# A new end, second-norm moments on VectorE and routing counts one step earlier, in an S4D plus mixture-of-experts kernel

## The reference

```python
x = x + _layernorm(_L0_attn_ref(_layernorm(x, axis=-1), ...), axis=-1)   # four S4D layers
x = x + _layernorm(_L0_ffn_ref(_layernorm(x, axis=-1), w1, w2, router_w), axis=-1)
```

## Time and profile before

| | us |
|---|---|
| median of the runs | 1039.69 |
| the three runs | 1039.56, 1039.69, 1178.92 |
| the profiled execution, device time | 1034.42 |
| its span, first to last instruction | 1032.6 |

### The profile page before, as it was taken

The page is one execution under the profiler, slowest core; times in us unless marked ns, Lnnn a source line. Parts: engine busy times, 40 slices in busy tenths (PEclk is TensorE's granted clock), DMA queues, the critical chain, the costliest instruction groups (busy, mean ns, idle before and its releaser), DMA issues.

```text
span 1032.6 us, 25421 instructions
## 1 busy us (share of the span) xinstructions
PE 689.0 (67%) x8355; PEld 594.1 (58%) x8356; DVE 746.7 (72%) x1806; ACT 574.8 (56%) x1249; POOL 553.6 (54%) x759
## 2 busy tenths in 40 slices
PE   0029438697677958789487888736999999990000
PEld 0018338675676738767386666635888898880000
DVE  8987866779675885759767599844778777773563
ACT  7627961069401792028700488824888888872544
POOL 2113314346441573415543277876777777777883
PEclk9999759899797988979798898557999999995555
DMA  7905699990999819995499400113555555542232
GB/s 282 397 0 161 201 386 388 330 385 4 312 387 324 303 48 358 384 329 205 140 361 403 176 1 1 62 52 118 163 165 168 167 161 168 163 143 56 79 97 74
DMA packets 123814, 209.13 MB, mean 203 GB/s; under 512 B 18892, under 2 KB 45784, under 8 KB 123096
## 3 DMA queue, kind: packets, MB, share of 16 engines
q1 hardware_dynamic: 115544, 191.28, 52.6%
q0 software_dynamic: 8192, 16.79, 5.6%
HBM read 168.97 MB, written 39.06 MB: 201 GB/s over the span
## 4 chain that ended last, share of the span: by engine, by line
POOL 30%; PE 28%; issue 26%; DVE 9%; ACT 4%; DMA 2%; POOLq 1%; SPq 0%; ACTq 0%; DVEq 0%
PE bank L1117 12%; POOL zbuf L561 7%; POOL toep L627 6%; PE bank L1132 6%; POOL rstd_of L550 6%; PE bank L970 3%; POOL z_sorted L613 3%; PE bank L948 2%; PE bank L1084 2%; POOL sums L541 1%; DMA toep<-kernels_dram 1%; POOL rstd_of L528 1%; POOL mean_of L546 1%; POOL m L548 1%; POOL shift_of L552 1%
## 5 line engine op out<-in xcount | busy, mean ns | idle before, releaser
L970 PE MATMUL bank<-zbuf,toep 128*128 128x128 f16 (+3 forms) x3328 | 145.4, 206 | 93.5 <-DVE zbuf L1327 72.2
L970 PEld LDWEIGHTS bank<-zbuf,toep 128*128 128x128 f16 x3328 | 142.0, 102 | 97.6 <-issue 50.6
L561 POOL TENSOR_TENSOR zbuf<-zbuf,w_cur 128x256 f32<-128x256 f32 x120 | 90.4, 755 | 141.2 <-DVE zbuf L1391 141.2
L613 POOL DMA_INDIRECT z_sorted<-toep x128 | 131.1, 1024 | 43.5 <-issue 35.3
L1117 PE MATMUL bank<-toep 128*128 128x256 f16 x1152 | 144.0, 275 | 3.1 <-issue 0.9
L1391 DVE TENSOR_REDUCE zbuf<-bank 128x256 f32<-128x512 f32 x128 | 86.9, 687 | 72.0 <-PE bank L970 72.0
L1005 PE MATMUL bank<-wo_cur,glu_work 128*128 128x256 f32 x512 | 135.6, 410 | 2.5 <-ACT glu_work L785 2.2
L785 ACT ACTIVATE glu_work<-bank,unscale_cur 128x512 f32<-128x512 f32 x64 | 42.7, 668 | 164.7 <-PE bank L992 164.6
L1117 PEld LDWEIGHTS bank<-toep 128*128 x1152 | 111.1, 99 | 22.3 <-issue 9.3
L1005 PEld LDWEIGHTS bank<-wo_cur,glu_work 128*128 128x128 f32 x512 | 97.2, 200 | 43.7 <-issue 17.8
L528 POOL TENSOR_TENSOR rstd_of<-var,neg_half 128x16 f32<-128x16 f32 (+1 forms) x16 | 37.6, 2352 | 106.8 <-DVE var L1187 106.6
(11 more groups left out here) (241 smaller groups left out, 1527.2 us busy)
## 6 DMA issues: line engine op xcount, KB each, us to landing
toep<-kernels_dram SPq DMA_DIRECT2D x104, 1024.0 KB, 14.0
glu_work<-kernels_dram SPq DMA_DIRECT2D x16, 1024.0 KB, 14.1
z_sorted<-ln_tmp SPq DMA_DIRECT2D x4, 3072.0 KB, 23.8
toep<-z_sorted SPq DMA_DIRECT2D x96, 128.0 KB
y_sorted<-toep SPq DMA_DIRECT2D x96, 128.0 KB
toep_last<-kernels_dram SPq DMA_DIRECT2D x8, 1024.0 KB, 14.2
hres<-in_x SPq DMA_DIRECT2D x1, 4096.0 KB, 13.0
toep<-in_x SPq DMA_DIRECT2D x1, 4096.0 KB, 23.9
```

The source lines that it names most:

```text
L561: G.tensor_tensor(y, y, w, ALU.mult).then_inc(s_yw, 1)
L613: nc.gpsimd.indirect_dma_start(out=z_sorted[c][:, :], out_offset=bass.IndirectOffsetOnAxis(ap=slot[:, k, t:t + 1], axis=0), in_=ybuf[:, t, ...
L970: last = MM(dst[:, d * (B // 4):, :], toep_slot(g)[:, c, d * P:(d + 1) * P, k], z_conv[:, 0:QUADS - d * (B // 4), g * GROUP + c].rearrange ...
```

## The change

1. POOL: all pacing (`after_a_tile`) goes. Scatters and gathers follow each other with the waits for their data alone. Its six last roots between gathers and the two after them go too.
2. The work after the gathers runs in seven pieces instead of eight equal parts: 16, 16, 16, 8, 4, 2 and 2 tiles. The order on VectorE per piece i is weighted_sum(i), last_shift(i), result(i-1).
3. Weights: ScalarE's multiplication by the first weight goes. VectorE forms y1 + y2 * exp(difference of logits) and normalizes that. Since LayerNorm doesn't see a common factor but for epsilon, epsilon is multiplied by the square of the sum of exponentials (`eps_of`).
4. The root of the last norm is a Sqrt on ScalarE followed by a reciprocal on VectorE.
5. The second norm's moments of quads 8 to 15 (chunks 2 and 3) move from POOL to VectorE: `z2_moments(c)`, one call for a chunk, in VectorE's steps 16 and 20 after add_x. The root is a seed from the bits of the number (two conversions) and three Newton steps.
6. POOL's order becomes h0, h1, h2, z0, h3, z1, h4, z2, h5, z3, h6, four scatters, h7, 28 scatters.
7. `count(c)` on TensorE moves from step 15 + 4c to 14 + 4c (the last one stays behind the loop), `places(c)` on VectorE from 16 + 4c to 15 + 4c.

The diff, cut:

```diff
+Z2_BY_DVE = 2
+
+PIECES = [(c * CHUNK, CHUNK) for c in range(CHUNKS - 1)] + [(48, 8), (56, 4), (60, 2), (62, 2)]
...
-            def after_a_tile(last):
-
-                paced[0] += 1
-                pool.wait_ge(s_xT, min((paced[0] + 1) // 2, last))
...
             h_moments(0)
             h_moments(1)
-            for u in range(2, len(PAIRS)):
+
+            for u in range(2, 6):
                 h_moments(u)
                 z2_moments(u - 2)
+            h_moments(6)
             scatter(0, range(0, 4))
-            z2_moments(len(PAIRS) - 2)
-            scatter(0, range(4, 8))
-            z2_moments(len(PAIRS) - 1)
-            scatter(0, range(8, 32))
+            h_moments(7)
+            scatter(0, range(4, 32))
             for c in range(1, CHUNKS):
-                scatter(c, last_tile=FIRSTS[c])
...
-            r = 0
-            for p in range(NORMS - 2, NORMS):
-                for k in range(2):
-                    for at_t in range(0, PART, 4):
-                        gather(p, k, at_t, 4)
-                        if r < NORMS - 2:
-                            last_root(r)
-                            r += 1
-            for r in range(NORMS - 2, NORMS):
-                last_root(r)
+                scatter(c)
+
+            for i, (first, n) in enumerate(PIECES):
+                if first == TILES - CHUNK:
+                    for c in range(CHUNKS):
+                        pool.wait_ge(s_scat[c], 16 * 2 * CHUNK)
+                gather(i)
...
-                act.wait_ge(s_z2_in, q // 2 + 1)
+                if q < Z2_BY_DVE * 4:
+                    act.wait_ge(s_z2_in, q // 2 + 1)
+                else:
+                    act.wait_ge(s_z2_dve, q // 4 - Z2_BY_DVE + 1)
...
+            for i, (first, n) in enumerate(PIECES):
+                act.wait_ge(s_var, 2 * CHUNKS + i + 1)
+                A(all_tiles(rstd_of)[:, first:first + n], var[:, 0:n], ACT.Sqrt).then_inc(s_root, 1)
+                act.wait_ge(s_last_in, i + 1)
+                for t in range(first, first + n):
+                    y1 = y_of(0, t)[:, 0, :]
+                    A(y1, y1, ACT.Identity, scale=all_tiles(rstd_of)[:, t:t + 1],
+                      bias=all_tiles(shift_of)[:, t:t + 1]).then_inc(s_last, 1)
...
-                    c, at_c = divmod(q - 15, 4)
+                    c, at_c = divmod(q - 14, 4)
...
+            def z2_moments(c):
...
+                dve.wait_ge(s_z2_in, Z2_BY_DVE * 2)
+                dve.wait_ge(s_bn2, (c + 1) * CHUNK)
+                st.done(TT(z2_sums, z2_stats[:, :, 1:3], z2_stats[:, :, 4:6], ALU.add))
+                st.done(TT(z2_diff, z2_stats[:, :, 1], z2_stats[:, :, 4], ALU.subtract))
+                st.after()
...
+                st.done(V.tensor_copy(z2_diff, z2_m2.bitcast(I32)))
+                st.after()
+                st.done(TS(rstd_c.bitcast(I32), z2_diff, -0.5, ROOT_SEED, ALU.mult, ALU.add))
+                st.after()
+                for _ in range(3):
+                    st.done(TT(z2_diff, rstd_c, rstd_c, ALU.mult))
+                    st.after()
+                    st.done(STT(z2_diff, z2_diff, -0.5, z2_m2, ALU.mult, ALU.mult))
+                    st.after()
+                    st.done(STT(rstd_c, z2_diff, 1.5, rstd_c, ALU.add, ALU.mult))
+                    st.after()
+                TT(shift_c, mean_c, rstd_c, ALU.mult).then_inc(s_z2_dve, 1)
...
+                    if q - 5 in range(Z2_BY_DVE * 4 + 3, QUADS, 4):
+                        z2_moments((q - 5) // 4)
...
-                c, at_c = divmod(q - 16, 4)
+                c, at_c = divmod(q - 15, 4)
...
+            def weighted_sum(i):
+
+                first, n = PIECES[i]
+                mean_i = all_tiles(mean_of)[:, first:first + n]
+                dve.wait_ge(s_gath[i], 16 * 2 * n)
+                for t in range(first, first + n):
+                    y1, y2 = (y_of(k, t)[:, 0, :] for k in range(2))
+                    st.done(STT(y1, y2, top[:, 1, t:t + 1], y1, ALU.mult, ALU.add))
+                st.after()
+                for k in range(n):
+                    st.done(V.bn_stats(stats[:, k, :], y_of(0, first + k)[:, 0, :]))
...
+                if i > 0:
+
+                    dve.wait_ge(s_root, i)
+                TT(var[:, 0:n], m2[:, 0:n], diff[:, 0:n], ALU.add).then_inc(s_var, 1)
...
+                dve.wait_ge(s_root, i + 1)
+                st.done(V.reciprocal(rstd_i, rstd_i))
+                st.after()
+                STT(shift_i, mean_i, -1.0, rstd_i, ALU.mult, ALU.mult).then_inc(s_last_in, 1)
...
+                TT(hres[:, tiles, :], y_of(0, first, n), hres[:, tiles, :], ALU.add).then_inc(s_res, 1)
+            for i in range(len(PIECES)):
+                weighted_sum(i)
+                last_shift(i)
+                if i > 0:
+                    result(i - 1)
+            result(len(PIECES) - 1)
```

More of the change, by code:

```diff
@@ L60 @@
 WORK_SLOTS = 8
+Z2_BY_DVE = 2
+PIECES = [(c * CHUNK, CHUNK) for c in range(CHUNKS - 1)] + [(48, 8), (56, 4), (60, 2), (62, 2)]
+assert sum(n for _, n in PIECES) == TILES
 WEIGHT_STEPS = (19, 20, 22)
@@ L159, in build @@
         mean = sb("mean", [P, CHUNK])
-        sums, z2_sums = (sb(name, [P, CHUNK, 2]) for name in ("sums", "z2_sums"))
+        sums, z2_sums = (sb(name, [P, CHUNK, 2])[:, :, :] for name in ("sums", "z2_sums"))
         diff = sb("diff", [P, CHUNK])
@@ L495, in _ @@
                 store(SEGS - 1, n, n % RING)
-            for p in range(NORMS):
-                tiles = slice(p * PART, (p + 1) * PART)
-                sp.wait_ge(s_res, p + 1)
+            for i, (first, n) in enumerate(PIECES):
+                tiles = slice(first, first + n)
+                sp.wait_ge(s_res, i + 1)
                 sp.dma_start(out[:, tiles, :], hres[:, tiles, :]).then_inc(s_out, 16)
-            sp.wait_ge(s_out, 16 * NORMS)
+            sp.wait_ge(s_out, 16 * len(PIECES))
         @block.gpsimd
@@ L595, in z2_moments, with scatter @@
                 moments_of(last_layer, PAIRS[u], z2_stats, z2_sums, z2_diff, z2_m2, s_z2_in)
-            paced = [0]
-            def after_a_tile(last):
-                paced[0] += 1
-                pool.wait_ge(s_xT, min((paced[0] + 1) // 2, last))
-            def scatter(c, which=range(2 * CHUNK), last_tile=None):
+            def scatter(c, which=range(2 * CHUNK)):
                 pool.wait_ge(s_slots, c + 1)
@@ L615, in scatter, with gather @@
                         in_=ybuf[:, t, :], in_offset=None).then_inc(s_scat[c], 16)
[L617 to L623, removed]
[L624 to L629 removed]
+            def gather(i):
+                first, n = PIECES[i]
+                g = SEG_OF[first // CHUNK]
+                if first == SEGMENTS[g][0] * CHUNK:
+                    for m in range(RING):
+                        pool.wait_ge(s_yt[m], 16 * ((FIRSTS[g] + XTS[g]) // RING))
+                for k in range(2):
+                    for t in range(first, first + n):
+                        nc.gpsimd.indirect_dma_start(
+                            out=y_of(k, t)[:, 0, :], out_offset=None, in_=y_sorted[g][:, :],
+                            in_offset=bass.IndirectOffsetOnAxis(ap=slot[:, k, t:t + 1], axis=0)).then_inc(s_gath[i], 16)
@@ L1666, in last_shift @@
[L1666 to L1680 removed]
+            token_sums()
@@ new lines, in last_shift, with result @@
+            def last_shift(i):
+                first, n = PIECES[i]
+                rstd_i, mean_i, shift_i = (all_tiles(buf)[:, first:first + n] for buf in (rstd_of, mean_of, shift_of))
+                dve.wait_ge(s_root, i + 1)
+                st.done(V.reciprocal(rstd_i, rstd_i))
+                st.after()
+                STT(shift_i, mean_i, -1.0, rstd_i, ALU.mult, ALU.mult).then_inc(s_last_in, 1)
+            def result(i):
+                first, n = PIECES[i]
+                tiles = slice(first, first + n)
+                dve.wait_ge(s_last, first + n)
+                TT(hres[:, tiles, :], y_of(0, first, n), hres[:, tiles, :], ALU.add).then_inc(s_res, 1)
```

98 lines of the change are left out of this document (30 added, 68 removed).

## The result

The changed kernel takes 1001.75 us as the median of four runs (997.38 to 1003.32), the kernel before 1039.86 beside it: ratio 0.9638, 95% interval 0.9602 to 0.9674, 3.6% less. The profiled execution took 1002.86, its span is 1001.0 (before: 1032.6). The part that the change doesn't touch happened to be 4.7 us later in this trace (`h_moments(6)` starts on POOL at 637.25, before at 632.55). So stretches are compared, not readings of the time. Three single executions, 1178.92 of the kernel before and 1811.54 and 2420.33 in one experiment (`e1_before_unpaced`), are left out of all ratios; no profile caught one.

The account below looks back on a forecast made before the run. POOL, late rather than held back, was taken to bound the kernel: 7.9 + 2.0 + 4.6 + 11.2 - 0.9 = 24.8, plus 11.1 after the last gather, 35.9 off. That gave 1003.8, the forward sum 998.3; forecast 1004.5, range 995 to 1017.

Parts of the forecast that it names:

- First scatter: POOL's first scatter: earlier `places(0)` and moments moved to VectorE let it start at 641.0, 7.9 us earlier.
- First 32 scatters: POOL's scatters up to the 33rd: 2.0 us saved among the first eight, 4.6 by pacing gone, 6.6 in all.
- Roots: Six Pows between POOL's last gathers, priced at 1.87 each: 11.2 us saved by moving them off POOL.
- Results against gathers: VectorE's result additions stretching POOL's gathers at the end: 5.4 us before, 6.3 after, so 0.9 lost.
- Sums against gathers: VectorE's runs of weighted sums beside POOL's gathers at the end: the forecast had no term for them.
- TensorE's start and the experts' end: Expert stage: TensorE starts near 697, held by the slots, and ends 223 us later at 920.
- After the last gather: From the last gather to the end of the span: 10.3 us instead of 21.4, 11.1 saved.
- the forward sum: Second count, adding POOL's pieces and the tail forward from the first scatter at 641.0: 998.3.
- rival A: End of the kernel: experts and VectorE bound it, not POOL; about 1012 in the median's terms; chance 12%.
- B: POOL beside long VectorE instructions: fewer blocks than charged, the 4.8 and 6.3 vanish, 994; chance 8%.
- C: Expert stage: scatters running ahead collide with expert loads; at 0.05 more for each of 224, 1016; chance 8%.
- D: Expert stage: TensorE at half clock, 446 us instead of 223, whole about 1230, slower than before; chance 2%.

Follow-up runs that it names:

- e1_before_unpaced: The kernel before with its pacing alone taken out: 1033.93 us against 1035.04, ratio 0.9948.
- e2: The changed kernel with the old front (all second-norm moments on POOL in its old order, count and places a step later): 1013.54 us, ratio 0.9775.
- e6: The changed kernel with the pacing of scatters and of the first 96 gathers put back: 1008.07 us, ratio 0.9711.
- e8: The changed kernel with six Pows of 8 columns, which nothing waits for, put among POOL's last 32 gathers: 1012.01 us, ratio 0.9749.
- e9: The changed kernel with 50 unread bn_stats (about 10 us) added on VectorE behind the token sums: 1002.29 us, ratio 0.9658.
- e3: The changed kernel with all second-norm moments back on POOL in its old order, count and places still a step earlier: 1018.89 us, ratio 0.9814.
- e4: The changed kernel with count and places moved back a step, moments of chunks 2 and 3 still on VectorE: 1011.51 us, ratio 0.9728.
- e5: The changed kernel with eight equal pieces of eight tiles in place of 16, 16, 16, 8, 4, 2, 2: 999.00 us, ratio 0.9633.
- the four variants: e7, e10, e11 and e12, run on another chip where the kernel before takes 1097.16 us: all 12 to 14% slower than before.
- e7: The changed kernel with each result written as one addition per tile: 1232.2 us, ratio 1.1211 to the kernel before on another chip.
- e10: The changed kernel with each `low_weights` cut into eight operations of 256 columns: 1231.0 us, ratio 1.1212 to the kernel before on another chip.
- e11: The changed kernel with weighted sums and bn_stats in turn: 1225.74 us, ratio 1.1171 to the kernel before on another chip.
- e12: The changed kernel with results by tile, low_weights in eight and sums and bn_stats in turn: 1245.53 us, ratio 1.1363 to the kernel before on another chip.

## Why the prediction was right

The forecast was 1004.5; 1001.75 was measured, and the stretches sum to 36.2 where 35.9 was said. The mechanism held step by step: POOL is late, not held back, so whatever leaves it or comes earlier on it reaches the end nearly in full (e2, e6 and e8 show it one by one, e9 the other side of it). That the sum came out to 0.3 us is luck: gathers gained 2.7 less than said, the first scatters 1.7 and the tail 2.2 more, 0.9 went elsewhere, and the part ahead of the change alone moves by up to 9 us between runs. The terms:

- **First scatter**: -7.9 said, -7.7 measured; e3 and e4 show that the step's two halves can't be priced apart.
- **First 32 scatters**: 8.3 instead of 6.6. The three `low_weights` cost 3.5 in place of 4.8, since a stall depends on where in the instruction the scatter begins, and the first four scatters nearly nothing over their usual pitch (1.2 said).
- **Roots**: 11.2 was too much. The term forgot that the 0.30 between gathers is there anyway; 9.4 without it.
- **Results against gathers**: 6.3 said, 3.8 measured (0.95 + 0.94 + 1.28 + 0.62). The gather that began 0.02 before a result took 0.94 (943.80); the next began 1.2 into it. On average I had them 0.6 in.
- **Sums against gathers**: put at nothing, 3.3 us measured (928.53, 937.17, 954.75 at 2.06, 2.59, 1.52). Before, beside runs of eight, a gather took 1.12 at most; I priced only instructions that are long by themselves. Together both kinds cost 7.1, against 5.4 before: 1.7 lost instead of 0.9. In four other traces with the same pieces (e2, e3, e4, e6) they cost 8.4 to 8.5.
- **TensorE's start and the experts' end**: 697 and 920 said, 695.3 and 919.9 after taking off the 4.7; `z2_moments` took 3.6 and 3.4 where 3.2 was said. The stage lasted 224.7, so one of the prediction's signs of being wrong, over 223, came true; VectorE's slack covered it.
- **After the last gather**: 8.1 instead of 10.3. Landing (1.6) and computing (4.0; 4.2 said) were right; the store was said to take 4.6 as in the earlier trace rows and took 2.5. The size is the smaller part of it: e5 stores as much as before and takes 3.0 from its last result's end (993.41) to its span's. What else was in before's 4.6 stays open.
- **Arithmetic**: the forward sum comes to 998.1, not 998.3, and rival A's own numbers (938 + 54 + 7 = 999) give 1006 in the median's terms, not 1012. At 1006 a time could hardly have told A from the forecast; the waits of VectorE did.

Of the rivals, A fell with e9; B did not come (the two kinds of stall that it would have struck out cost 3.5 and 7.1), though e5 shows that with other instants those at the end nearly vanish; C was not seen on the first two chips, where the scatters ran at 1.318 unpaced and 1.313 paced. D's end result, slower than before with TensorE at half clock, is what the four variants show on the last chip, but not by its mechanism, a busy TensorE at half clock: the granted clock is 0.50 in those windows, and TensorE is busy for only 14 of the 120 us. I had looked at what unpaced scatters do to POOL and to the transfers, not at what they may do to the other engines.

## What to carry to other kernels

Find the engine that is late without a break, and price each edit by what it removes from that engine's row; an instruction among evenly spaced ones costs itself less the gap that was there anyway. Look also at what an instruction releases on other engines: before, five of the six roots on POOL started the very result that then held up POOL's next gather. Where a step needs two things at once, move both or neither: here one alone gained 0.5 us or lost 3.1 up to the first scatter, and both gained 7.7. Before taking a pacing out for 4 to 8 us, time it on more than one chip: here variants without it stood 2 to 4% below the kernel before on two chips and 12 to 14% above it on a third (that the pacing is the reason is not shown).

## What was not expected of the hardware

**VectorE's runs of short instructions hold up POOL's indirect DMAs.** In the changed kernel each of the 16-sum runs stretches one gather to 1.52 to 2.59 us, ending 0.8 us after the run does (937.17 + 2.59 = 939.76; the run ends at 938.94). A long instruction does the same (945.05 + 1.89 = 946.94; it ends at 946.13). Breaking a long one into pieces back to back helps at some instants and not at others: in e7 two runs of 16 one-tile additions stretched no gather and a third one to 2.33; beside eight pieces of a `low_weights` (e10) a scatter took at most 1.22. Sums with a bn_stats between them stretched none over 1.3 (e11, e12). What decides which gather of a run is caught stays open. The Trainium skill (SBUF — State Buffer, on what shares a port between VectorE and GpSimd) infers that a tensor_tensor leaves descriptor writing alone; the rows of L1699 show 0.6 to 1.3 us each.

**A chip on which the other engines stand still.** With POOL issuing one indirect DMA per 1.26 us, TensorE, VectorE and ScalarE stood still together on one chip for 26 to 57 us at a time, at 15 to 17% DMA load, and not at all in the traces from two others with the same scatters. The kernel before takes 1097 on that chip, 57 more than its 1040 elsewhere; no trace shows where. The cause stays open.
